# A mixture-of-experts decoder kernel: the experts' rows are gathered by a table of token numbers instead of being scattered into slots

## The reference, cut to what matters

```python
xf = layernorm(x).reshape(T, H)
scores = softmax(xf @ w_cls.T)                       # [T, 64]
_, topk_idx = top_k(scores + bias, K)
w = normalized scores of the chosen
routed = topk_idx < E
order = argsort(flat_ids)                            # by expert, then by token
pos = arange(N) - starts[ids_s]                      # place within the expert
buf = zeros((E, CAP, H)).at[ids_s, pos].set(x_exp[order], mode='drop')
gu = einsum('ech,ehf->ecf', buf, w_gate_up)
g, u = split(gu, 2, axis=-1)
y = einsum('eci,eih->ech', silu(g) * u, w_down)
...
out = sum over the K choices of w * y[expert, pos]   # choices with pos >= CAP give 0
```

## Time and profile before

| what | us |
|---|---|
| runs (lowest, median, highest) | 3036.84, 3042.47, 3046.91 |
| the profiled execution | 3039.41 |
| its span | 3037.4 |
| PE, DVE, ACT, POOL busy | 2468.5, 1837.5, 1242.0, 855.3 |
| mean granted TensorE clock | 0.899 |
| POOL's 128 scatters L2248: busy, and issue time ahead of them | 135.6, 40.1 |
| the load of an expert's rows on SP, issue to landing (median) | 4.6 |
| the loads of its weights, 1 MB and 512 KB | 5.6, 6.5 |

### The profile page before, as it was taken

How to read it: one execution, slowest core, us unless ns; L and a number is a source line. 1 busy time by engine, 2 the same in 40 slices (tenths; PEclk the granted TensorE clock), 3 DMA queues, 4 the chain that set the end, 5 groups by cost and what they waited for, 6 DMA issues and landing times. The chain is left out here.

```text
span 3037.4 us, 34907 instructions
## 1 busy us (share of the span) xinstructions
PE 2468.5 (81%) x12662; PEld 1636.9 (54%) x12662; DVE 1837.5 (60%) x2917; ACT 1242.0 (41%) x1873; POOL 855.3 (28%) x1198
## 2 busy tenths in 40 slices
PE   5898989863443356999448999999999869999999
PEld 4454545321221135999334554545555538888887
DVE  3766576627888964777557777565655544444443
ACT  2444444328656624666203433344333323333332
POOL 2232222215578773333443332001211110000000
PEclk8999999976665677999768999999999979999999
DMA  3213131227122245999585656333433323101000
GB/s 117 64 43 84 43 84 46 70 77 287 62 97 92 84 161 180 305 304 303 173 182 138 157 147 156 88 89 100 113 95 92 102 85 133 42 1 42 1 28 14
DMA packets 200952, 340.40 MB, mean 112 GB/s; under 512 B 28809, under 2 KB 60425, under 8 KB 198754
## 3 DMA queue, kind: packets, MB, share of 16 engines
q1 hardware_dynamic: 177250, 299.80, 32.5%
q0 software_dynamic: 20480, 37.87, 5.1%
q10 hardware_dynamic: 3072, 0.79, 0.1%
HBM read 182.30 MB, written 109.05 MB: 96 GB/s over the span
## 5 line engine op out<-in xcount | busy, mean ns | idle before, releaser
L757 DVE TENSOR_REDUCE at_negmax<-at_ps 128x2 f32<-128x1024 f32 (+3 forms) x256 | 259.1, 1016 | 120.7 <-PE at_ps L523 63.7
L670 ACT ACTIVATE at_probs<-at_ps 128x1024 f32<-128x1024 f32 (+3 forms) x256 | 221.7, 866 | 269.9 <-PE at_ps L538 267.6
L1367 DVE TENSOR_REDUCE a_negmax<-a_ps 128x2 f32<-128x1024 f32 x128 | 155.1, 1217 | 137.0 <-PE a_ps L1120 136.4
L1896 ACT ACTIVATE gr_act_signs<-gr_signed,gr_test 128x512 bf16<-128x512 f32 x248 | 177.2, 716 | 81.5 <-POOL gr_test L2236 53.4
L59 PE MATMUL ff_ps<-ff_xnT_hi,ff_s_hi 128*128 128x512 f32 x512 | 201.1, 393 | 5.1 <-DVE ff_xnT_lo L2766 5.1
L61 PE MATMUL ff_ps<-ff_xnT_hi,ff_s_lo 128*128 128x512 f32 x512 | 200.4, 391 | 0.0
L60 PE MATMUL ff_ps<-ff_xnT_lo,ff_s_hi 128*128 128x512 f32 x512 | 200.4, 391 | 0.0
L538 PE MATMUL at_ps<-at_qk 98*128 98x512 f32 (+3 forms) x512 | 172.1, 418 | 21.2 <-DMA at_qk<-at_mrow 11.5
L2796 DVE TENSOR_TENSOR ff_hid<-ff_hid,ff_ps 128x512 f32<-128x512 f32 x64 | 44.0, 688 | 238.6 <-ACT ff_hid L2741 238.6
L1268 ACT ACTIVATE a_probs<-a_ps 128x1024 f32<-128x1024 f32 x128 | 130.9, 1023 | 135.1 <-PE a_ps L1138 134.6
L518 PE MATMUL at_ps<-at_qk 96*128 96x512 f32 (+3 forms) x512 | 162.4, 381 | 19.5 <-DVE at_xnT_lo L818 8.9
(11 more groups left out here) (410 smaller groups left out, 6557.1 us busy)
## 6 DMA issues: line engine op xcount, KB each, us to landing
at_qk<-at_part SPq DMA_DIRECT2D x384, 128.0 KB, 2.5
first_gu<-in_L_ffn_w_gate_up_dram SPq DMA_DIRECT2D x32, 1024.0 KB, 5.6
a_qk<-a_part SPq DMA_DIRECT2D x192, 128.0 KB, 2.3
slot_rows<-gr_zeros SPq DMA_DIRECT2D x16, 1024.0 KB
first_d<-in_L_ffn_w_down_dram SPq DMA_DIRECT2D x32, 512.0 KB, 6.5
ex_rows<-slot_rows SPq DMA_DIRECT2D x32, 512.0 KB, 4.6
out_rows<-ex_y SPq DMA_DIRECT2D x32, 512.0 KB, 3.1
gr_aside_raw<-in_L_ffn_W_dram SPq DMA_DIRECT2D x48, 256.0 KB, 3.1
```

The lines of the kernel that those rows point to most:

```text
L670: act.activation(probs[:, t % 2, 2 * w:2 * w + 2, lo:S], banks(("kq", g, s), lo), ACT.Exp, scale=SCALE).then_inc(free(("kq", g, s)), 1)
L757: dve.reduce_max(negmax[:, g % 2, :].rearrange("p (j t) -> p j t", t=NT)[:, 2 * w:2 * w + 2, t], banks(("qk", g, s), 0, width(g, t)), AX.X ...
L1367: dve.reduce_max(negmax[:, g % 2, :].rearrange("p (j t) -> p j t", t=NT)[:, 2 * w:2 * w + 2, t], banks(("qk", g, s)), AX.X, negate=True).t ...
L1896: act.activation(act_signs[:, j, :], src, ACT.Sign, scale=-1.0, bias=against, accum_out=total[:, i, j:j + 1]).then_inc(counted_to[j], 1)
```

## The change: what it does

The normed rows are stored once, in the order of the tokens, to `normed` [T+1, D] (four stores of 1 MB by SP; row 0 is zero). No row is scattered, and there is no zero fill of slots. Instead the kernel computes `index` [128, 64]: for each slot the number of its token plus one, or 0.

- DVE `places` decodes each place into a block of 32 and a row within it, `row[token, expert]` (0 where the expert is not chosen), in four small operations a batch.
- POOL makes `rows_hot` (32 comparisons of 128x128, three beside each counting round from round 23 on, the rest after the rounds) and `block_hot` (eight comparisons, then two products of 128x1024 by the number of the tile and by that of the token in it). For the last batch DVE makes `rows_hot` in one comparison of 128x4096.
- PE `table` multiplies the two, 32 bf16 products a batch, whose sum over tokens leaves in each place the one token number that belongs there. DVE `add_table` adds the batches; PE `move_tokens` brings the numbers to the partitions that the gather wants; DVE writes `index`.
- In the experts, SP no longer loads rows. POOL gathers them, two indirect DMAs of 128 rows an expert, by `index`.
- `rstds(b-1, 1)` stands in round 7 of every batch (before in round 8 for batch 1 and in round 5 for the later ones). `hot` is bf16; the gate weights are summed in two halves; some tiles share room.

The diff, cut to its core:

```diff
-            many = slot_rows.rearrange("(p q r) d -> q p (r d)", p=P, r=zeros.shape[1] // D)
-            for q in range(ZERO_DMAS):
-                sp.dma_start(many[q], zeros[:]).then_inc(zeroed, 16)
-            sp.dma_start(none_row, zeros[0:1, 0:D]).then_inc(zeroed, 16)
+            for dst in (none_row, normed[0:1, :]):
+                sp.dma_start(dst, zeros[0:1, 0:D]).then_inc(zeroed, 16)
+            normed_tiles = normed[1:T + 1, :].rearrange("(b t p) d -> b p t d", p=P, t=NT)
+
+            def store_normed(b):
+                sp.wait_ge(xn_done, NT * (b + 1))
+                sp.dma_start(normed_tiles[b], xn[:, b % 2]).then_inc(normed_out, 16)
...
+            def table(b):
+                pe.wait_ge(logT_copied, b + 1)
+                pe.wait_ge(blocks_set, b + 1)
+                if b < B - 1:
+                    pe.wait_ge(rows_set, ROW * (b + 1))
+                else:
+                    pe.wait_ge(vector_rows, 1)
+                for t in range(NT):
+                    for g in range(GROUPS):
+                        e = SIDE * g
+                        mm = pe.matmul(ps[:, LOGT, g * P // 2:(g + 1) * P // 2], rows_hot[:, t, e:e + SIDE, :].rearrange("p e r -> p (e r)"),
+                                       block_hot[:, :, t, e:e + SIDE, :], start=t + g == 0, stop=t == NT - 1 and g == GROUPS - 1, skip_group_check=True)
+                mm.then_inc(tabled, 1)
+
+            def move_tokens():
+                pe.wait_ge(index_step, 1)
+                by_side = token_of[:].rearrange("p g (t w) -> p w g t", w=SIDE)
+                for h in range(SIDE):
+                    for w in range(SIDE):
+                        mm = pe.matmul(ps[ROW * w:ROW * (w + 1), MOVED, h * GROUPS * HALVES:(h + 1) * GROUPS * HALVES], env.ident[:, ROW * h:ROW * (h + 1)],
+                                       by_side[:, w], start=True, stop=True, skip_group_check=True)
+                mm.then_inc(moved, 1)
...
+            def add_table(b):
+                dve.wait_ge(tabled, b + 1)
+                for h in range(SIDE):
+                    here = slice(ROW * h, ROW * (h + 1))
+                    new = ps[here, LOGT, :].rearrange("p (g n h k) -> p h g n k", n=2, h=SIDE, k=BLOCKS)[:, h]
+                    if b:
+                        dve.tensor_tensor(found[here], found[here], new, ALU.add).then_inc(tab_added, 1)
+                    else:
+                        dve.tensor_copy(found[here], new).then_inc(tab_added, 1)
...
+                    flat, chosen = place[:].rearrange("p t e -> p (t e)"), mask[:].rearrange("p t e -> p (t e)")
+                    dve.tensor_scalar(row[:], flat, 1.0 / ROW, 0.5 / ROW - 0.5, ALU.mult, ALU.add).then_inc(decoding, 1)
+                    dve.wait_ge(decoding, DECODE * b + 1)
+                    dve.tensor_scalar(block_of[:], row[:], 1.5 * 2.0 ** 23, 1.5 * 2.0 ** 23, ALU.add, ALU.subtract).then_inc(decoding, 1)
+                    dve.wait_ge(decoding, DECODE * b + 2)
+                    dve.scalar_tensor_tensor(out=row[:], in0=block_of[:], scalar=-float(ROW), in1=flat, op0=ALU.mult, op1=ALU.add).then_inc(decoding, 1)
+                    dve.wait_ge(decoding, DECODE * b + 3)
+                    dve.scalar_tensor_tensor(out=row[:], in0=row[:], scalar=1.0, in1=chosen, op0=ALU.add, op1=ALU.mult).then_inc(decoding, 1)
...
-                for part in (gate_weights, slot_numbers) if b < B - 1 else (slot_numbers, gate_weights):
+                for part in (gate_weights, places, slot_numbers) if b < B - 1 else (places, last_rows, slot_numbers, gate_weights):
...
-            def scatter(b, lo, hi):
-                for at in range(lo, hi):
-                    if at == 0:
-                        pool.wait_ge(slots_done, 2 * b + 1)
-                        pool.tensor_tensor(pool_carrier[:, b:b + 1], env.minus_half[:, 0:1], env.minus_half[:, 0:1], ALU.mult)
-                    n = b * NT * TOPK + at
-                    pool.indirect_dma_start(slot_rows, bass.IndirectOffsetOnAxis(slots[:, n:n + 1], 0), xn[:, b % 2, at // TOPK, :], None,
-                                            bounds_check=SLOTS - 1, oob_is_err=False).then_inc(scattered[b % 2], 16)
+            def row_hot(b, n):
+                if n == 0:
+                    pool.wait_ge(decoding, DECODE * (b + 1))
+                    if b:
+                        pool.wait_ge(tabled, b)
+                pool.tensor_scalar(rows_hot[:].rearrange("p t e r -> p (t e) r")[:, :, n], row[:], n + 1.0, None, ALU.is_equal).then_inc(rows_set, 1)
+
+            def blocks_hot(b):
+                pool.wait_ge(decoding, DECODE * (b + 1))
+                if b:
+                    pool.wait_ge(tabled, b)
+                for n in range(BLOCKS):
+                    pool.tensor_scalar(in_block.rearrange("p (e k) -> p e k", k=BLOCKS)[:, :, n], block_of[:], float(n), None, ALU.is_equal).then_inc(numbers, 1)
+                pool.wait_ge(numbers, (BLOCKS + 1) * b + BLOCKS)
+                pool.tensor_tensor(block_hot[:, 1].rearrange("p t e k -> p t (e k)"), in_block.rearrange("p (t m) -> p t m", t=NT),
+                                   bcast_last(tile_no[:, NT * b:NT * (b + 1)], NT, E_ROUTED * BLOCKS), ALU.mult).then_inc(numbers, 1)
+                pool.wait_ge(numbers, (BLOCKS + 1) * (b + 1))
+                pool.tensor_scalar(in_block, in_block, token[:, 0:1], None, ALU.mult).then_inc(blocks_set, 1)
...
-            LATE = 22
-            EARLY = {0: 2, 4: 5, 5: 1, 7: 1, 9: 3, 10: 1, 11: 2, 13: 2, 15: 1, 17: 1, 18: 1, 20: 1, 21: 1}
-            assert sum(EARLY.values()) + TESTS - LATE == NT * TOPK
             for b in range(B):
-                sent = TESTS - LATE
                 for r in range(TESTS):
                     for j in range(COUNTED[b]):
                         update(b, r, j)
-                    if b and r == (8 if b == 1 else 5):
+                    if b and r == 7:
                         rstds(b - 1, 1)
-                    if b >= 2 and r in EARLY:
-                        scatter(b - 2, sent, sent + EARLY[r])
-                        sent += EARLY[r]
-                    if 0 < b < B - 1 and r >= LATE:
-                        if b == 1 and r == LATE:
-                            pool.wait_ge(zeroed, 16 * (ZERO_DMAS + 1))
-                        scatter(b - 1, r - LATE, r - LATE + 1)
+                    if b and r >= WRITE_AT:
+                        for v in range(A_ROUND * (r - WRITE_AT), A_ROUND * (r - WRITE_AT + 1)):
+                            row_hot(b - 1, v)
+                if b:
+                    for v in range(A_ROUND * (TESTS - WRITE_AT), ROW):
+                        row_hot(b - 1, v)
+                    blocks_hot(b - 1)
                 rstds(b, 0)
-            scatter(B - 2, 0, 12)
             rstds(B - 1, 1)
-            scatter(B - 2, 12, NT * TOPK)
-            scatter(B - 1, 0, NT * TOPK)
-            for i in range(2):
-                pool.wait_ge(scattered[i], 16 * NT * TOPK * B // 2)
...
-                turned[u].wait(sp, i, 0)
-                sp.dma_start(rows[:, u], rows_dram[bass.ds(e, 1)].rearrange("e p t d -> (e p) t d")).then_inc(rows_in[u].sem, 16)
...
+            def gather(e):
+                i, u = e // 2, e % 2
+                turned[u].wait(pool, i, 0)
+                for t in range(CT):
+                    at = CT * (E_ROUTED // SIDE * (e % SIDE) + e // SIDE) + t
+                    pool.indirect_dma_start(rows[:, u, t, :], None, normed, bass.IndirectOffsetOnAxis(index[:, at:at + 1], 0)).then_inc(rows_in[u].sem, 16)
+
+            gather(0)
+            gather(1)
             split_d(0, 0)
             split_d(0, 1)
+            gather(2)
             for e in range(E_ROUTED):
+                if e + 3 < E_ROUTED:
+                    gather(e + 3)
                 if e + 2 < E_ROUTED:
                     split_d(e // 2 + 1, e % 2)
```

117 lines of the change are left out of this document (89 added, 28 removed).

## The result

| | before | changed |
|---|---|---|
| median of the runs, us | 3041.34 (4 runs) | 3156.12 (3152.91 to 3156.88, 4 runs) |
| the profiled execution's span, us | 3037.4 | 3154.3 |
| ratio | 1 | 1.0374, interval 1.0355 to 1.0394 |

The change makes the kernel 3.7% slower, 115 us; the forecast was 3065, 24 us slower, with 3095 as its upper end. The direction was right, the size was not. Of the 91 us that the forecast missed, 67 lie in the graph stage and 21 in the experts; the chain in the experts (+73.3) alone outweighs the shorter seam (-17.1), so the direction was not luck, but the largest miss has the other sign than its forecast. The first thing to do with such a result is to lay the stage borders of the two traces beside each other. I take four points: the last `normalize` of the graph stage on DVE, the first turn of the experts on PE, the first load of the stage after, and the end.

What follows compares the result with a forecast made beforehand. PE was taken to bound the experts, while no engine was full in the graph stage. From 3039.4 us, -26.4 (shorter seam) + 3.3 + 36.4 + 12.6 = +25.9 gave 3065, range 3020 to 3095.

Steps and rivals of the forecast that it cites:

- Part 1: Graph stage up to the last normalize: scatters and zero fill removed, decoding and table sums added on DVE, -6.9 us.
- The expected relief of -14.2: DVE's waits at three graph-stage lines, tied to the removed scatters and zero fill, shrink by 14.2 us together.
- Rival (e): Graph stage: `blocks_hot` ahead of `rstds` and the table ahead of the adjacency give back the gain, +9, 3074; chance 0.05.
- cover: Graph stage: DVE's threshold work was taken to hide POOL's some 8 us of `blocks_hot` and the table on PE.
- Part 2: Tail from the last normalize to the experts' first turn: DVE work +10.4, first turn at 1139.1 in place of 1165.5.
- Part 3: Experts' start: the third expert's rows, gathered behind both first splits, come late, +3.3 us.
- Part 4: Experts' steady state: gathers behind a POOL split come 2.6 us late on every second expert, 14 turns, +36.4 us.
- the three landings: Experts: gather landing times seen in the trace, 4.2 to 4.5, 5.8 to 6.3, and 7.4 to 8.0 us.
- the upper pair: Experts: the slower landings, favoured by 1.5 MB of weights issued at the very moment of the gathers.
- Part 5: Experts: PE's granted clock falls after the pauses, 0.9 us for each of 14, +12.6 us, ends 0 and 48.

Runs made afterwards that it cites:

- Run 4: Changed kernel plus 16 POOL comparisons of 128x128 in four output forms at the graph stage's start: 1.05 us each with stride 32 or 8, 0.59 without a gap.
- Run 12: Kernel before plus 20 unused POOL comparisons after the counting rounds of batches 1, 2 and 3, ahead of `rstds(b, 0)`: 3091.49 us (1.0161).
- run 5: run 1 with `rows_hot` made by one DVE comparison of 128x4096 in every batch, POOL's 96 comparisons removed: 3034.25 us (0.9974); repeated, 3041.91 (0.9996).
- Run 8: Changed kernel with each pair of gathers in the experts issued one period earlier, at the same place behind a split: 3088.35 us (1.0145).
- the second run: Changed kernel with `rstds(b, 0)` issued right after the counting rounds, ahead of POOL's remaining one-hot work: 3163.76 us (1.0398).
- run 3: the second run with PE's table after the adjacency, `add_table` just before `normalize`, and `rstds(b, 1)` right after the one-hot work: 3141.36 us (1.0320).
- the best version: Changed kernel with `rows_hot` on DVE in every batch, gathers one period earlier and `gather(2)` between the first two splits: 3032.51 us (0.9965).
- run 1: Changed kernel with the experts' gathers issued ahead of the split they stood behind on POOL: 3094.05 us (1.0159).

## Why the prediction was wrong

**Part 1 failed, by 67 us.** The step reads: "POOL's new comparisons cost nothing in this sum, since the scatters that they replace took 1.27 us each ... and a comparison some 0.41". Two things were wrong in it. The price: some 1.0 (96 in 96.3 us) against 0.41, from a row of another operation with another output; I took the nearest row as the value, while a row whose output has no gap can only be a lower bound for one that has. Run 4 gives 0.59 for the cheap form and 1.05 for this one. And the place: I compared totals. In the loop POOL's one-hot work is 131 us (20.4, 8.5 and 5.7 for the blocks, and the first row below), and the scatters had 108.7 (second row, of the kernel before), 22 us less, which could not give +60:

```profile
L2347 POOL TENSOR_SCALAR gr_rows_hot<-gr_row 128x128 bf16<-128x128 f32 x96 | 96.3, 1027 | 7.1
```
```profile
L2248 POOL DMA_INDIRECT slot_rows<-shared_x,slots x77 | 84.0, 1090 | 24.7 <-issue 24.7
```

Most of the scatters stood between the rounds; 21.2 of the new work's 44 us a batch stand after the last round, where DVE, ACT and PE wait for what comes next. Run 12 turns such a wedge into 54 us without anything else; run 5 takes 32 us a batch away, and its last normalize is 53.6 us earlier than the changed kernel's, of the 60. The expected relief of -14.2 at L2051, L2126 and L2130 cannot be seen beside that. In the four traces with run 5's loop, where POOL is light, the last normalize is 6.7 to 14.2 us later than before, with 18 to 20 us more of work on DVE (362.9 to 364.7 us, before 344.7), so that the reliefs there pay for a part of what DVE got; how large a part, this scatter does not tell.

**Rival (e) was this mechanism**, with the right instructions in it (`blocks_hot` ahead of `rstds`, the table ahead of the adjacency), at +9 and a chance of 0.05. Its size rested on the same 0.41, and on cover for 5 of its 8 us: with 1.0 for a comparison, and the eight of `row_hot` that stand there too, 21 us less the same 5 would have given 3 x 16.

**Part 2 was right**: -17.1 from the last normalize to the first turn, forecast -19.5. The 128x4096 took 4.42 (4.6). That the sum comes so close is in part luck: `block_hot` was not in time, as part 2 had it, the table had to wait for it until 1186.3, and DVE's late units hid most of this.

**Part 3**: the third turn waited 4.1 us, forecast 3.3.

**Part 4 was right in its mechanism, small in its size.** 14 waits were forecast after the third turn and 14 came, on every second turn; they sum to 46.6, 3.3 each, for 2.6. Of the three landings the middle one (6.1) was taken, and 6.8 was measured, beside the weights as argued for the upper pair. The rule of the Trainium skill on how the engines go round the queues ("DMA: Bandwidth & Descriptors", "Queues, rings and completion order") would have had the landings at the lower end; what was measured lies between, so a gather of 256 KB beside 1.5 MB on another queue is slowed, but not put behind it. Run 8 shows that the landing alone does not make the waits: with the same landings and an earlier issue they are gone.

**Part 5 was half the size.** After 13 of the 14 waits PE needs 8.2 in place of 6.6 us, 13 x 1.6 = 20.8, and after the third turn 9.2, another 2.6: 23.4, for 12.6. With it the stage closes: 50.7 of waits and 23.4 of clock are 74.1, and 73.3 were measured. Less than half of such a stretch runs at the lower level (0.50 in the row from 1300.5 to 1303.5 above, 1.00 in those before and behind it), so that it loses 1.6 us and not the 3.4 of the earlier trace rows, where all of 6.8 us ran at 0.50. In the loop of which the Trainium skill tells in the section "HAM oscillation — how this bites in real kernels" (page "TensorE: Matmul & The Clock Gate"), the clock falls after every such wait; here it did after 13 of the 14.

What stays open: whether the second run is slower than the changed kernel at all (of the 5.1 us between the traces 4.1 lie in the experts, which it does not touch); how much of run 3's chain is POOL and how much the copies that the later table delays; why the experts take 331 us in one run and 337 in another of the same kernel; and by how much the best version beats the kernel before on other chips.

## What to carry to other kernels

When work is moved onto an engine that feeds several others, look at where in the period it stands, not at its total: write down who waits for the first thing behind it. Take the price of an operation from a row with the same form of output, and where there is none, carry the sum through with twice the value to see whether the answer turns. A transfer that is late by less than a period can be mended by issuing it a period earlier, at the same place, without making it faster (run 8); here that gave as much as moving it ahead of the split (run 1), for the two intervals overlap. And when an order of instructions is changed, look at what the moved work pushes, and whom that meets: in run 1 it was the split and not the gather that slowed DVE.

## What the runs showed of the hardware

- POOL's comparisons of 128x128, each waiting for the one before, follow each other in 0.59 us if the output has no gap and in 1.05 if it has one of 8 or 32 bf16 elements (run 4). Eight with a stride of 8 that do not wait took 7.11 us (0.89 each); of eight beside DVE's comparison of 128x4096 the first took 5.25 us and the others 0.96 each.
- DVE does the same 4096 columns in one operation in 4.42 us, 1.1 ns a column; POOL's 32 comparisons of 128 columns took 32 us.
- DVE's TENSOR_TENSOR of 128x512 (the low part), started while POOL's of 128x1024 (the split) runs, ends 0.5 to 0.6 us after it: 0.69 us became 1.53 (kernel before, 13 of 13 low parts) and 2.35 to 2.96 (run 1, 14 of 14). Beside POOL's issue of an indirect DMA it kept its 0.69.
- After a pause of 3.0 to 3.6 us PE's granted clock fell from 1.00 to 0.50 for a part of the next stretch in 13 of 14 cases, which then took 8.2 us in place of 6.6; once, after a pause of 3.12 us, it stayed at 1.00.
